# A four-layer cross-attention kernel: an earlier bias on GpSimd, a reordered layer 2, and the last layer's loads cut into pieces

## The chip, the cores and the metric

The kernel is one program on one core of a Trainium2 chip. The metric is the device time of one launch in microseconds (us), the median of several runs. TensorE (PE) does matmuls and transposes, VectorE (DVE), ScalarE (ACT) and GpSimd (POOL) do elementwise work, and SyncE (SP) issues nearly all transfers.

## The reference, cut to what matters

The model is four layers. Each adds a cross-attention and then a feed-forward block to an activation `x` of 16 x 64 rows of 512. Everything is float32.

```python
x = x + xattn0(layernorm(x), ctx)          # windowed attention
x = x + ffn0(layernorm(x))                 # int8-style SwiGLU
x = x + xattn1(layernorm(x), ctx)          # 32 heads of 128, 8 kv heads, rms norm of q and k
x = x + mxfp4(layernorm(x)) @ mxfp4(W).T + bias        # second ffn
x = x + xattn2(layernorm(x), ctx)          # 32 heads of 16, 64 queries and 64 keys a batch
x = x + topk_lora_ffn(layernorm(x))        # third ffn
x = x + xattn3(layernorm(x), cat(ctx, layernorm(x)))   # 16 heads of 96, 4 kv heads
x = x + layernorm(x) @ dequant3bit(q3, ranges).T + bias3
```

`mxfp4` takes blocks of 32 values, forms a power-of-two scale from the block's maximum and rounds each value to a 4-bit grid. `dequant3bit` is `q / 7 * (max - min) + min` with a (min, max) pair for every 32 weights. Softmax subtracts the row maximum, exponentiates and divides by the sum.

## The kernel before, in words

The activation lies in one buffer `X` of 8 tiles of 128 rows. All work is cut into *stages*: a stage has a name and an index, as `l2_s 3` for the scores of batch 3 of layer 2. `stage_order()` writes one list of all stages, `ORDER`. Each of the five engines walks through that same list and issues its own part of every stage. So the list fixes each engine's order, and the engines are bound together by semaphores alone. Every engine works in order: an instruction that waits holds up all that stands behind it on its engine.

- A matmul is three products of float32r parts, high x high, high x low and low x high. So every large weight is split after its load: ACT copies the high part (`high_parts`, L1607) and DVE subtracts it for the low part (`low_parts`, L1192).
- PSUM banks are handed out by `psum_uses`; a fill of a bank waits for the reads of the fill before it.
- **Second ffn (`f1_*`)**: for each tile DVE takes statistics, POOL makes the scale (L1979 to L1988), ACT writes the normalized rows `xn` (L1600), DVE quantizes them (`mxfp4`, nine instructions, L1197 to L1217), PE transposes (L664), ACT copies (L1807), PE multiplies (L891), and DVE adds to `X`. The bias is added to `X` on POOL (L2098). Then follow statistics, rows and transposes (L647) for layer 2. This pipeline runs beside the last steps of layer 1's attention and the first of layer 2's.
- **Layer 2's attention**: for each of 16 batches `l2_a` makes the masked keys on POOL (L2114), `l2_s` the scores on PE (L937, two banks) and on DVE the two maxima (L1432, L1435) and the subtraction for the first bank (L1440). `l2_e` exponentiates on ACT (L1853, L1860). `l2_z` takes sums and reciprocals on DVE (L1451, L1454) and multiplies on POOL (L2123). `l2_t` transposes on PE (L949), `l2_v` multiplies by the values (L960), and `l2_c` projects (L972), once for two batches. `pipe2` lists the stages of a step with their lag.
- **Layer 3's attention**: 32 units `i` (4 kv heads x 8 tiles). A step runs `l3_v i-2` (L847), `l3_a i` (L1078), `l3_t i-1` (L840), the exponentials, `l3_c i-3` (the projection, L857) and `l3_q` (a quarter of the query projections, L1059), five ahead. Heads of 96 leave quarters of partitions over, so after `l3_v` SP moves pieces inside SBUF (`o<-o`, three transfers) before `l3_c` may read. `w3` and `wo3` are the query and output weights of one kv head, 768 KB each.
- **Last ffn (`f3_*`)**: `q3`, `mn` and `mx` are its 3-bit weights and ranges. POOL rebuilds the weights piece by piece in `l3_c`, ACT and DVE split them.

SP's share of `l3_c` at index 0 is where the whole of the last ffn's inputs is issued:

```python
load(wo3[1], d["w3"][1][:, 1536:3072], D.wo3)
on.wait_ge(kv3_done.full, kv3_done.n + 1)
load(q3, d["q3"], D.f3)
for c in range(4):
    for k in range(2):
        load(range_rows(mn, c)[:, :, k, :], d["mn"][:, c, k], D.f3)
        load(range_rows(mx, c)[:, :, k, :], d["mx"][:, c, k], D.f3)
load(b3h, d["b3"], D.f3)
```

Of the kernel before, what the change touches and what calls it, by code (L numbers as in the profile page):

```python
# [17 lines left out]
NT = 8  # L18
# [42 lines left out]
def stage_order():  # L61
# [38 lines left out]
    def queries_at(u):  # L100
# [68 lines left out]
    for step, stages in enumerate(pipe2):  # L169
        order.extend(stages + kv.get(step, []))  # L170
# [24 lines left out]
def psum_uses(stage, i):  # L195
# [34 lines left out]
    if stage == "f1_turn":  # L230
        return [("p", (3,) if i < 6 else sh)]
    if stage == "f1_mm":
        return [("p", (7,) if i < 5 else sh)]
    if stage == "l2_turn":
        return [("p", (2,) if i < 4 else sh)]
# [117 lines left out]
def build_program(nc, d, out):  # L353
    ctx = ExitStack()
    with ctx:
# [42 lines left out]
        D.wo3, D.w3, D.f3, D.out = sem("d_wo3"), sem("d_w3"), sem("d_f3"), sem("d_out")  # L398
# [728 lines left out]
        def vector_program(v):  # L1127
# [295 lines left out]
            def l2_s(b):  # L1423
# [122 lines left out]
            def l3_c(i):  # L1546
# [4 lines left out]
                if 20 <= i < 24:  # L1551
                    j = i - 20
# [29 lines left out]
        def scalar_program(a):  # L1582
# [310 lines left out]
            def l3_keys(g):  # L1893
                if g == 2:
                    high_parts(w3h, w3[0], 3, D.w3, 16, S.w3h)
# [15 lines left out]
            def l3_main(_):  # L1911
                high_parts(woh3, wo3[0], 3, D.wo3, 16, S.wo3h)

            def l3_q(j):
# [11 lines left out]
                if part == 3 and g % 2 and g < 7:  # L1926
                    high_parts(w3h, w3[g // 2 + 1], 3, D.w3, 16 * (g // 2 + 2), S.w3h)
# [16 lines left out]
            def l3_c(i):  # L1944
                h, t = divmod(i, NT)
                if t == NT - 1 and h < 3:
                    w = PSUM["l3_c", i, "p"]
                    on.wait_ge(w.full, w.n + 1)
                    high_parts(woh3, wo3[h + 1], 3, D.wo3, 16 * (h + 2), S.wo3h)
                if 20 <= i < 24:  # L1950
# [494 lines left out]
```

## Time and profile before

| | us |
|---|---|
| median of 3 runs | 1686.17 (1682.86 to 1687.11) |
| the profiled execution's own time | 1683.93 |
| its span, first to last instruction | 1682.1 |
| PE busy | 1575.3 (94%) |
| DVE busy | 823.6 (49%) |
| ACT busy | 752.8 (45%) |
| POOL busy | 517.1 (31%) |
| mean granted TensorE clock | 0.979 |

A unit of PE's time that is not busy is a time in which PE stood with its next instruction still waiting. The granted clock is the share of full speed (2.4 GHz) that the chip let TensorE have; its other level is 1.2 GHz, so a mean of 0.9 over a stretch is a fifth of it at the lower level. In the profile a row names the engine, the line of the kernel, the operation, what it writes and reads, and in brackets how long the engine had been idle before it and who ended that.

### The profile page before, as it was taken

Reading aid. Unit: us, or ns where it says so; the run is one execution under the profiler, and the core shown is the slowest. Engines: PE = TensorE matmul, PEld = TensorE weight load, DVE = VectorE, ACT = ScalarE, POOL = GpSimd, SP = SyncE. Lnnn points to the kernel's source line nnn. Section 1 sums busy time; section 2 is a strip of 40 time slices with the busy share of each in tenths; the row PEclk is TensorE's granted clock in tenths of the full one; section 3 lists DMA queues with packets and bytes.
Section 4 is the critical chain, followed back from the end, with each engine's and each line's share of the span. In section 5 each row is a group of like instructions: output and inputs, shape, how many; then the busy total and the mean of one; then the engine's idle time right before and its main releaser. Section 6 shows DMA issues by size and latency. Waiting matters only on the chain. (4 is left out here: it accounts for less than half of the span.)

```text
span 1682.1 us, 25955 instructions
## 1 busy us (share of the span) xinstructions
PE 1575.3 (94%) x9522; PEld 1286.6 (76%) x9522; DVE 823.6 (49%) x1697; ACT 752.8 (45%) x2529; POOL 517.1 (31%) x648
## 2 busy tenths in 40 slices
PE   6999897789999999999999999779999999899998
PEld 5877776678888888888888888556555577787886
DVE  4566655354444454554444437755655312242454
ACT  3445443445454544544544455344333212454551
POOL 5666654132222222222222224333321000133323
PEclk9999999999999999999999999889999999999999
DMA  7000000102010010101010110011000001320101
GB/s 235 15 7 8 7 1 13 51 1 94 26 39 26 8 39 19 39 26 39 26 38 26 39 51 1 29 44 38 8 1 0 25 5 51 108 60 21 43 21 57
DMA packets 42942, 58.22 MB, mean 35 GB/s; under 512 B 26064, under 2 KB 33616, under 8 KB 39872
## 3 DMA queue, kind: packets, MB, share of 16 engines
q1 hardware_dynamic: 41136, 56.05, 10.4%
q8 instruction: 76, 1.25, 0.3%
q10 hardware_dynamic: 1616, 0.51, 0.1%
q14 instruction: 50, 0.41, 0.1%
q0 software_dynamic: 64, 0.00, 0.0%
HBM read 48.94 MB, written 2.10 MB: 30 GB/s over the span
## 5 line engine op out<-in xcount | busy, mean ns | idle before, releaser
L1727 ACT ACTIVATE big<-pb 128x128 f32<-128x128 f32 x384 | 106.6, 278 | 310.1 <-PE pb L793 202.7
L2089 POOL TENSOR_TENSOR big<-big 128x512 f32<-128x512 f32 x96 | 99.9, 1041 | 274.4 <-DVE big L1376 274.0
L1778 ACT ACTIVATE big<-pb,big 128x128 f32<-128x128 f32 x384 | 136.1, 368 | 68.8 <-issue 43.7
L1371 DVE TENSOR_REDUCE big<-pb 128x4 f32<-128x512 f32 x96 | 65.9, 686 | 174.7 <-PE pb L832 167.4
L808 PE MATMUL pb<-wkh,CXh 128*128 128x256 f32 x512 | 149.5, 292 | 1.5 <-DVE big L1361 1.5
L808 PE MATMUL pb<-wkl,CXh 128*128 128x256 f32 x512 | 144.3, 282 | 0.0
L808 PE MATMUL pb<-wkh,CXl 128*128 128x256 f32 x512 | 143.6, 281 | 0.0
L2079 POOL TENSOR_SCALAR big<-big 128x6 f32<-128x6 f32 x64 | 13.0, 204 | 424.3 <-ACT big L1727 423.7
L1166 DVE TENSOR_TENSOR X<-X,pb 128x512 f32<-128x512 f32 x128 | 86.9, 679 | 87.5 <-PE pb L1014 36.0
L857 PE MATMUL pb<-woh,oh 128*128 128x512 f32 x256 | 113.1, 442 | 3.0 <-DVE wol L1192 2.9
L793 PE MATMUL pb<-wqh,CXh 128*128 128x512 f32 x256 | 103.1, 403 | 10.6 <-DVE wql L1192 5.1
L793 PE MATMUL pb<-wqh,CXl 128*128 128x512 f32 x256 | 102.1, 399 | 0.0
L793 PE MATMUL pb<-wql,CXh 128*128 128x512 f32 x256 | 102.0, 398 | 0.0
L857 PE MATMUL pb<-woh,ol 128*128 128x512 f32 x256 | 101.7, 397 | 0.0
L857 PE MATMUL pb<-wol,oh 128*128 128x512 f32 x256 | 100.3, 392 | 0.0
L847 PE MATMUL pb<-big 128*128 128x256 f32 (+1 forms) x384 | 99.9, 383 | 0.0
L808 PEld LDWEIGHTS pb<-wkh,CXh 128*128 128x128 f32 x512 | 96.6, 189 | 2.3 <-DVE big L1361 1.8
L808 PEld LDWEIGHTS pb<-wkh,CXl 128*128 128x128 f32 x512 | 96.8, 189 | 0.0
L808 PEld LDWEIGHTS pb<-wkl,CXh 128*128 128x128 f32 x512 | 96.5, 188 | 0.3 <-issue 0.2
L1361 DVE COPY big<-pb 128x512 f32<-128x512 f32 x56 | 38.7, 690 | 104.5 <-PE pb L820 104.0
L2084 POOL TENSOR_TENSOR big<-big,half 128x6 f32<-128x6 f32 x64 | 85.0, 1328 | 9.4
L857 PE MATMUL pb<-woh,o 128*128 128x512 f32 x192 | 71.6, 428 | 7.8 <-DMA o<-o 7.5
(256 smaller groups left out, 3922.0 us busy)
## 6 DMA issues: line engine op xcount, KB each, us to landing
big<-in_w SPq DMA_DIRECT2D x17, 1024.0 KB, 4.9
big<-in_w SPq DMA_DIRECT2D x8, 768.0 KB, 5.0
big<-in_w SPq DMA_DIRECT2D x8, 512.0 KB, 3.5
o<-o SPq DMA_DIRECT2D x96, 32.0 KB, 1.9
X<-in_x SPq DMA_DIRECT2D x8, 256.0 KB, 5.7
big<-in_cn SPq DMA_DIRECT2D x8, 256.0 KB, 2.7
CXlf<-in_cT SPq DMA_DIRECT2D x8, 256.0 KB, 5.3
big<-in_wa SPq DMA_DIRECT2D x1, 2048.0 KB, 8.0
```

Of the source, the lines that this page charges most:

```text
L793: a = pe.matmul(bank(p), x_rows(x, c, t), y[:, 512 * c:512 * c + 512], start=(n == 0), stop=(n == 11))
L808: a = pe.matmul(bank(p)[:, s * 256:s * 256 + 256], kv_rows(x, c, 2 * t + s), y[:, 256 * c:256 * c + 256], start=(n == 0), stop=(n == 11), ...
L847: a = pe.matmul(bank(p)[0:hd, s * 256:s * 256 + 256], v_of(s), pt[:, s * 256:s * 256 + 256], start=(s == 0), stop=True, skip_group_check=True)
L857: a = pe.matmul(bank(p), x[:, 128 * c:128 * c + 128], y[:, 512 * c:512 * c + 512], start=(n == 0), stop=(n == 3 * size - 1))
L1166: v.tensor_tensor(X[:, t, :], X[:, t, :], bank(p), ADD).then_inc(p.free, 1)
L1361: v.tensor_copy(QT[i % 2].rearrange("p (b h q) -> p h b q", b=2, h=4), bank(p).rearrange("p (h b q) -> p h b q", h=4, b=2)).then_inc(p.fre ...
L1371: v.tensor_reduce(m[j % 2], quarters(bank(p)), AX, MAX, negate=True).then_inc(S.m, 1)
L1727: y = a.activation(sq[i % 2], bank(p)[:, j * width:j * width + 128], ACT.Square, accum_out=ss[i % 2][:, first + j:first + j + 1])
L1778: y = a.activation(e_[:, c], bank(p)[:, c], ACT.Exp, bias=m[j % 2][:, k:k + 1], scale=1.0, accum_out=z[j % 2][:, k:k + 1])
L2079: g.tensor_scalar(ss[i % 2][:, 0:6], ss[i % 2][:, 0:6], 1.0 / 128, 1e-6, MUL, ADD).then_inc(*on.to(S.pool))
L2084: g.tensor_tensor(rr[i % 2][:, 0:6], ss[i % 2][:, 0:6], half[:, 0:6], ALU.pow).then_inc(*on.to(S.rr))
L2089: g.tensor_tensor(quarters(e_), quarters(e_), bc(r[j % 2], 128), MUL).then_inc(*on.to(S.pn))
```

## The change

1. The bias of the second ffn on POOL waits until ACT has written the tile's rows, no longer until DVE has quantized them. The pipeline of that ffn gets an empty stage, `f1_wait`, between the quantizing and its transpose.
2. In layer 2 `l2_z` moves from the head of a step to behind `l2_s`, and the second ffn's step from ahead of `l2_a` to behind it. Inside `l2_s` DVE takes the first bank's maximum, subtracts, and then takes the second bank's maximum. A few PSUM tables follow.
3. `l3_turn` goes behind the values and keys of its step in layer 3's start.
4. The loads of 768 KB become three of 256 KB each, issued in several steps. The last ffn's inputs are loaded in four groups over sixteen steps, not at once, and its weights are rebuilt two steps later.
5. Layer 3's queries run six steps ahead, and the last ffn's stages are woven in after two stages of a step.

```diff
-    f1 = ["f1_stats", "f1_norm", "f1_quant", "f1_turn", "f1_mm", "l2_stats", "l2_rows", "l2_turn"]
-    ffn1 = pipeline([2 * t for t in range(NT)], [(s, every) for s in f1], ("f1_quant",))
+    f1 = ["f1_stats", "f1_norm", "f1_quant", "f1_wait", "f1_turn", "f1_mm", "l2_stats", "l2_rows", "l2_turn"]
+    ffn1 = pipeline([2 * t for t in range(NT)], [(s, None if s == "f1_wait" else every) for s in f1], ("f1_quant",))
...
-    pipe2 = batch_steps(16, [("l2_z", 3, every), ("f2_rows", 7, odd), ("l3_rows", 12, odd), ("f2_o", 11, odd),
+    pipe2 = batch_steps(16, [("f2_rows", 7, odd), ("l3_rows", 12, odd), ("f2_o", 11, odd),
...
-                             ("l2_v", 5, every), ("l2_t", 4, every), ("l2_s", 2, every), ("ffn1", 0, every),
-                             ("l2_a", 1, every), ("l2_e", 2, every), ("l2_q", 0, queries_at), ("f2_a", 8, odd),
+                             ("l2_v", 5, every), ("l2_t", 4, every), ("l2_s", 2, every), ("l2_z", 3, every),
+                             ("l2_a", 1, every), ("ffn1", 0, every), ("l2_e", 2, every), ("l2_q", 0, queries_at), ("f2_a", 8, odd),
...
-        order.extend(stages + kv.get(step, []))
+        turns = [s for s in stages if s[0] == "l3_turn"]
+        order.extend([s for s in stages if s not in turns] + kv.get(step, []) + turns)
...
-    order.extend([("l3_q", 4), ("l3_keys", 3)])
+    order.extend([("l3_q", 4), ("l3_q", 5), ("l3_keys", 3)])
...
-        if step + 5 < 4 * NT:
-            stages.append(("l3_q", step + 5))
+        if step + 6 < 4 * NT:
+            stages.append(("l3_q", step + 6))
...
-            together(stages, (ffn3, 0), (ffn3, len(stages)))
+            together(stages, (ffn3, 2), (ffn3, len(stages)))
...
                 on.mark(v.tensor_reduce(m2[2 * b % 4], b0, AX, MAX, negate=True))
-                first = on.n
-                on.wait_ge(p1.full, p1.n + 1)
-                v.tensor_reduce(m2[(2 * b + 1) % 4], b1, AX, MAX, negate=True).then_inc(S.m2, 1)
...
-                on.wait_ge(S.dve, first)
+                on.wait_ge(S.dve, on.n)
                 v.tensor_tensor(sm[2 * b % 6].rearrange("p (g k) -> p g k", g=8), b0, bc(m2[2 * b % 4], 64),
                                 ADD).then_inc(p0.free, 1)
+                on.wait_ge(p1.full, p1.n + 1)
+                v.tensor_reduce(m2[(2 * b + 1) % 4], b1, AX, MAX, negate=True).then_inc(S.m2, 1)
...
             def f1_quant(t):
-                on.wait_ge(S.mx4, 4 + t + 1)
+                rows_made(on, "f1", t)
...
+            def load_piece(h, k):
+
+                dst, landed = (w3, D.w3) if k < 3 else (wo3, D.wo3)
+                load(dst[h][:, 512 * (k % 3):512 * (k % 3) + 512], d["w3"][h][:, 512 * k:512 * k + 512], landed)
...
+                if part < 3 and g in (2, 4):
+                    on.wait_ge(S.w3l, 3 * (g // 2 + 1))
+                    load_piece(g // 2 + 1, part)
...
+                if h < 3 and 3 <= t < 6:
+                    on.wait_ge(S.wo3l, 3 * (h + 1))
+                    load_piece(h + 1, t)
+
+                j, part = divmod(i - 2, 4)
+                if 0 <= j < 4:
                     on.wait_ge(kv3_done.full, kv3_done.n + 1)
...
+                    if part == 0:
+                        load(q3[:, 512 * j:512 * j + 512], d["q3"][:, 512 * j:512 * j + 512], D.f3[j])
+                    elif part < 3:
                         for k in range(2):
...
+                            if part == 1:
+                                load(range_rows(mn, j)[:, :, k, :], d["mn"][:, j, k], D.f3[j])
+                            else:
+                                load(range_rows(mx, j)[:, :, k, :], d["mx"][:, j, k], D.f3[j])
```

Lines of the kernel after the change stand two further down than before in TensorE's part and up to `mxfp4`, and one further down in most of ACT's and POOL's.

How the order moves, at three places. First POOL, where layer 2 begins; `L2098` (after: `L2099`) is the bias of the ffn's last tile, `L2114` (`L2115`) the masked keys, `L2123` (`L2124`) the multiplication of `l2_z`. Before:

```order
467 L2114 TENSOR_TENSOR big<-big 128x256 [waits ln_rstd,d_masks,bank1_free]
468 L2098 TENSOR_TENSOR X<-X,big 128x512 [waits l2_k_masked,mxfp4]
469 L2114 TENSOR_TENSOR big<-big 128x256 [waits x_bias]
470 L2123 TENSOR_TENSOR big<-big 128x512 [waits l2_k_masked,l2_reciprocal]
471 L2123 TENSOR_TENSOR big<-big 128x512 [waits l2_probs,l2_reciprocal]
```

POOL at the same place after the change:

```order
464 L2115 TENSOR_TENSOR big<-big 128x256 [waits ln_rstd,d_masks,bank1_free]
465 L2115 TENSOR_TENSOR big<-big 128x256 [waits l2_k_masked]
466 L2099 TENSOR_TENSOR X<-X,big 128x512 [waits l2_k_masked,ln_rows_act]
467 L1980 TENSOR_SCALAR ve<-mv 128x1 [waits x_bias,ln_stats]
468 L1983 TENSOR_TENSOR rs<-ve,half 128x1 [waits pool_step]
469 L1989 TENSOR_SCALAR ve<-mv,rs 128x1 [waits pool_step]
470 L2124 TENSOR_TENSOR big<-big 128x512 [waits ln_rstd,l2_reciprocal]
471 L2124 TENSOR_TENSOR big<-big 128x512 [waits l2_probs,l2_reciprocal]
472 L2115 TENSOR_TENSOR big<-big 128x256 [waits l2_probs,bank2_full]
```

The second batch's keys now stand ahead of the last bias, and that bias waits for the rows (`ln_rows_act`) in place of the quantizing (`mxfp4`). From the third batch on the keys stand behind two multiplications whose sums come after the scores.

Second, DVE from the sums of batch 0 to the scores of batch 1, before:

```order
1089 L1451 TENSOR_REDUCE big<-big 128x8 [waits l2_exp]
1090 L1454 RECIPROCAL big<-big 128x8 [waits dve_step]
1091 L1451 TENSOR_REDUCE big<-big 128x8 [waits bank2_free]
1092 L1454 RECIPROCAL big<-big 128x8 [waits dve_step]
1093 L1432 TENSOR_REDUCE big<-pb 128x8 [waits bank1_full]
1094 L1435 TENSOR_REDUCE big<-pb 128x8 [waits bank2_full]
1095 L1440 TENSOR_TENSOR big<-pb,big 128x512 [waits dve_step]
```

The same two stages after the change:

```order
1088 L1434 TENSOR_REDUCE big<-pb 128x8 [waits bank1_full]
1089 L1439 TENSOR_TENSOR big<-pb,big 128x512 [waits dve_step]
1090 L1442 TENSOR_REDUCE big<-pb 128x8 [waits bank2_full]
1091 L1452 TENSOR_REDUCE big<-big 128x8 [waits l2_exp]
1092 L1455 RECIPROCAL big<-big 128x8 [waits dve_step]
1093 L1452 TENSOR_REDUCE big<-big 128x8 [waits bank2_free]
1094 L1455 RECIPROCAL big<-big 128x8 [waits dve_step]
```

The sums of one batch now follow the maxima of the next one, and the subtraction that releases the first exponential stands between the two maxima.

Third, SP in layer 3, where `o_0` and `o_1` are the moves after `l3_v`, `in_w` a weight load and `in_q`, `in_mn`, `in_mx` the last ffn's inputs. Before (the `in_mn` and `in_mx` rows go on to 16, then `in_b`, then the next `o_0`):

```order
93 L2174 DMA big<-in_w 128x1536 [waits w3_low]
94 L2174 DMA o_1<-o_1 32x2x128 [waits bank5_free]
95 L2174 DMA o_1<-o_1 32x2x128 x2
96 L2174 DMA big<-in_w 128x1536 [waits wo3_low]
97 L2174 DMA big<-in_q 128x2048 [waits bank3_full]
98 L2174 DMA CXhf<-in_mn 128x2x128
99 L2174 DMA CXlf<-in_mx 128x2x128
```

SP over the same units after the change:

```order
96 L2176 DMA big<-in_w 128x512 [waits w3_low]
97 L2176 DMA o_1<-o_1 32x2x128 [waits bank5_free]
98 L2176 DMA o_1<-o_1 32x2x128 x2
99 L2176 DMA big<-big 32x8x64 [waits bank0_free]
100 L2176 DMA big<-in_w 128x512
101 L2176 DMA o_0<-o_0 32x2x128 [waits bank5_free]
102 L2176 DMA o_0<-o_0 32x2x128 x2
```

Between the moves of two units there is now one piece of a weight and one query move, where eighteen issues of the last ffn's inputs and a whole weight stood.

## Rows read from the trace of the kernel before

**Rows 1.** Busy time by stretch: start:end length, PE, PEld, DVE, ACT, POOL, clock, DMA, GB/s.
```profile
1010.00:1104.00 94.00, 81.80 (x435) 66.34 (x435) 62.89 (x126) 44.17 (x132) 33.91 (x59) 0.93 0.04 13
1104.00:1166.00 62.00, 47.76 (x269) 32.58 (x266) 40.41 (x90) 29.72 (x92) 24.06 (x33) 0.89 0.09 35
1166.00:1360.00 194.00, 193.14 (x815) 109.86 (x814) 96.42 (x262) 63.43 (x162) 36.48 (x63) 1.00 0.04 14
...
1460.00:1520.00 60.00, 53.13 (x261) 43.76 (x260) 20.97 (x38) 27.20 (x91) 17.63 (x16) 0.90 0.21 57
...
1620.00:1682.10 62.10, 52.59 (x248) 40.78 (x247) 31.16 (x59) 15.31 (x49) 21.07 (x27) 0.97 0.13 44
```

**Rows 2.** PE's waits in all: line <- releaser: us in total, times, longest.
```profile
PE pb L937 <- POOL big L2114: 10.5, 2, 7.8
PE pb L857 <- DMA o<-o: 7.5, 4, 4.4
...
PE pb L664 <- DVE big L1217: 7.3, 4, 3.5
...
PE pb L647 <- ACT xn L1600: 5.1, 4, 1.4
```

**Rows 3.** Timeline of PE: one group of 32 query matmuls, twice (start, length, row).
```profile
1093.44 9.61 PE L916 MATMUL pb<-CXhf,big 128*128 128x256 f32 x32
...
1165.89 7.07 PE L916 MATMUL pb<-CXhf,big 128*128 128x256 f32 x32
```

**Rows 4.** Timeline of POOL and PE where layer 2 begins.
```profile
1111.59 1.26 POOL L2098 TENSOR_TENSOR X<-X,big 128x512 f32<-128x512 f32 x1 [13.90 <-DVE big L1217]
1112.93 0.61 POOL L2114 TENSOR_TENSOR big<-big 128x256 f32<-128x256 f32 x1
1113.60 2.08 PE L937 MATMUL pb<-big,CXlf 64*128 64x256 f32 x8 [7.82 <-POOL big L2114]
```

**Rows 5.** Timeline from one batch's scores to the next one's, PE, DVE and ACT.
```profile
1125.90 1.14 PE L937 MATMUL pb<-big,CXlf 64*128 64x256 f32 x8
1127.07 0.69 DVE L1432 TENSOR_REDUCE big<-pb 128x8 f32<-128x512 f32 x1 [6.04 <-PE pb L937]
1128.28 0.68 DVE L1440 TENSOR_TENSOR big<-pb,big 128x512 f32<-128x512 f32 x1
1129.53 1.73 ACT L1860 ACTIVATE big<-pb,big 128x64 f32<-128x64 f32 x8
1131.40 1.13 PE L937 MATMUL pb<-big,CXlf 64*128 64x256 f32 x8 [1.69 <-ACT big L1860]
```

**Rows 6.** Timeline later in layer 2: sums on DVE, POOL's multiplications, PE's light step.
```profile
1200.71 0.68 DVE L1451 TENSOR_REDUCE big<-big 128x8 f32<-128x512 f32 x1
1201.77 2.23 POOL L2123 TENSOR_TENSOR big<-big 128x512 f32<-128x512 f32 x2 [7.45 <-DVE big L1454]
1209.33 1.14 PE L937 MATMUL pb<-big,CXlf 64*128 64x256 f32 x8
1215.09 1.09 PE L949 MATMUL pb<-ident,big 128*128 128x128 f32 x8
1216.12 1.13 PE L937 MATMUL pb<-big,CXlf 64*128 64x256 f32 x8
```

**Rows 7.** Timeline of SP and PE in layer 3's attention.
```profile
1450.60 0.43 SPq L2174 DMA_DIRECT2D big<-in_q  x1
1462.60 1.87 SPq L2174 DMA_DIRECT2D o<-o  x3
1465.81 0.79 PE L857 MATMUL pb<-woh,o 128*128 128x512 f32 x1 [4.43 <-DMA o<-o]
1515.67 0.79 PE L857 MATMUL pb<-woh,o 128*128 128x512 f32 x1 [1.97 <-DMA o<-o]
```

**Rows 8.** DMA issues: count, KB each, median us from issue to landing.
```profile
big<-in_w SPq DMA_DIRECT2D x8, 768.0 KB, 5.0
...
o<-o SPq DMA_DIRECT2D x96, 32.0 KB, 1.9
```

More of the change, by code:

```diff
@@ L397, in build_program @@
         D.q3, D.o3 = [[sem(f"d_{n}3_{k}") for k in range(2)] for n in "qo"]
-        D.wo3, D.w3, D.f3, D.out = sem("d_wo3"), sem("d_w3"), sem("d_f3"), sem("d_out")
+        D.wo3, D.w3, D.b3, D.out = sem("d_wo3"), sem("d_w3"), sem("d_b3"), sem("d_out")
+        D.f3 = [sem(f"d_f3_{k}") for k in range(4)]
         banks = [ctx.enter_context(nc.psum_tensor(f"pb{i}", [128, 1024], F32)) for i in range(4)]
@@ L1948, in l3_c @@
                     on.wait_ge(w.full, w.n + 1)
-                    high_parts(woh3, wo3[h + 1], 3, D.wo3, 16 * (h + 2), S.wo3h)
-                if 20 <= i < 24:
-                    j = i - 20
+                    high_parts(woh3, wo3[h + 1], 3, D.wo3, 48 * (h + 2), S.wo3h)
+                if 22 <= i < 26:
+                    j = i - 22
                     on.wait_ge(S.w3f, j + 1)
@@ L2128, in l3_c @@
             def l3_c(i):
-                if 4 <= i < 20:
-                    j, part = divmod(i - 4, 4)
+                if 6 <= i < 22:
+                    j, part = divmod(i - 6, 4)
                     w = w3f[:, 512 * j:512 * j + 512]
                     low = range_rows(mn, j)
-                    on.wait_ge(D.f3, 288)
+                    on.wait_ge(D.f3[j], 80)
                     on.wait_ge(*on.last)
@@ L2147, in l3_c @@
                         g.tensor_tensor(w, w, low, ADD).then_inc(*on.to(S.w3f))
-                if i == 20:
+                if i == 22:
+                    on.wait_ge(D.b3, 16)
                     on.wait_ge(*on.last)
@@ L2269, in l3_begin @@
                 on.wait_ge(l2_done.full, l2_done.n + 1)
-                load(w3[0], d["w3"][0][:, 0:1536], D.w3)
+                for k in range(3):
+                    load_piece(0, k)
             def l3_keys(g):
@@ L2281, in l3_main @@
                 on.wait_ge(f2_done.full, f2_done.n + 1)
-                load(wo3[0], d["w3"][0][:, 1536:3072], D.wo3)
+                for k in range(3, 6):
+                    load_piece(0, k)
                 on.wait_ge(S.w3l, 3)
-                load(w3[1], d["w3"][1][:, 0:1536], D.w3)
+                for k in range(3):
+                    load_piece(1, k)
             def l3_q(j):
                 g, part = divmod(j, 4)
-                if part == 0:
-                    return
-                p, c = PSUM["l3_q", j - 1, "p"], part - 1
-                on.wait_ge(p.free, p.n + 1)
-                load(q3_heads(g, third(c))[:, :, 3, :], q3_heads(g, last)[:, :, c, :], D.q3[g % 2])
-                if part == 3 and g % 2 and g < 5:
-                    on.wait_ge(S.w3l, 3 * (g // 2 + 2))
-                    load(w3[g // 2 + 2], d["w3"][g // 2 + 2][:, 0:1536], D.w3)
+                if part:
+                    p, c = PSUM["l3_q", j - 1, "p"], part - 1
+                    on.wait_ge(p.free, p.n + 1)
+                    load(q3_heads(g, third(c))[:, :, 3, :], q3_heads(g, last)[:, :, c, :], D.q3[g % 2])
+                if part < 3 and g in (2, 4):
+                    on.wait_ge(S.w3l, 3 * (g // 2 + 1))
+                    load_piece(g // 2 + 1, part)
             def l3_v(i):
@@ L2306, in l3_c @@
                 h, t = divmod(i, NT)
-                if i == 0:
-                    on.wait_ge(S.wo3l, 3)
-                    load(wo3[1], d["w3"][1][:, 1536:3072], D.wo3)
+                if h < 3 and 3 <= t < 6:
[3 more added lines that the diff above has]
+                if 0 <= j < 4:
                     on.wait_ge(kv3_done.full, kv3_done.n + 1)
-                    load(q3, d["q3"], D.f3)
-                    for c in range(4):
+                    if part == 0:
+                        load(q3[:, 512 * j:512 * j + 512], d["q3"][:, 512 * j:512 * j + 512], D.f3[j])
+                    elif part < 3:
                         for k in range(2):
-                            load(range_rows(mn, c)[:, :, k, :], d["mn"][:, c, k], D.f3)
-                            load(range_rows(mx, c)[:, :, k, :], d["mx"][:, c, k], D.f3)
-                    load(b3h, d["b3"], D.f3)
-                if t == NT - 1 and h < 2:
-                    on.wait_ge(S.wo3l, 3 * (h + 2))
-                    load(wo3[h + 2], d["w3"][h + 2][:, 1536:3072], D.wo3)
+                            if part == 1:
+                                load(range_rows(mn, j)[:, :, k, :], d["mn"][:, j, k], D.f3[j])
+                            else:
+                                load(range_rows(mx, j)[:, :, k, :], d["mx"][:, j, k], D.f3[j])
+                if i == 18:
+                    load(b3h, d["b3"], D.b3)
             def end(_):
```

14 lines of the change are left out of this document (7 added, 7 removed).

## The prediction, made before the changed kernel was run

> **What bounds the kernel now.** I read the profile in this order: the page for the shares, busy time by stretch for where PE is idle, PE's waits for who ends them, and then timelines of the three places the change touches.
>
> PE is the bound. Of the 1682.1 us span it is busy 1575.3, and the change takes no matmul away. So only two things can be won: PE's idle time, and work done at TensorE's lower clock level. Both lie in few places [rows 1]. From 1010 to 1104 us (the second ffn beside the end of layer 1) PE is idle for 94.0 - 81.8 = 12.2 us at a granted clock of 0.93. From 1104 to 1166 (start of layer 2) it is idle for 14.2 us at 0.89. From 1166 to 1360 only 0.9 us is idle, at 1.00: nothing to win there, only to lose. From 1460 to 1520 (layer 3) it is idle 6.9 us at 0.90, and in the last 62 us for 9.5 us. The waits have names [rows 2]: PE's scores of layer 2 wait 10.5 us for POOL's masked keys, the projection of layer 3 waits 7.5 us for moves inside SBUF, the ffn's transposes wait 7.3 us for DVE's quantizing, and the transposes of normalized rows 5.1 us for ACT.
>
> What the lower level costs is seen directly: 32 equal matmuls took 9.61 us right after a wait and 7.07 us at full clock [rows 3]. A granted clock of c over a stretch loses at most (1 - c) of it; PE being busy only a share of the stretch, I count that share.
>
> **Part 1, the quantizing gets a step of slack (1010 to 1104 us).** The transpose of a tile stood one step behind its quantizing and waited 7.3 us in 4 waits [rows 2]. Now a step of PE work of several us lies between. DVE is busy 62.9 of the 94 us [rows 1], so it can follow a faster PE, though not by much more. Gone: 7.3 us. About 1.0 of the row waits (5.1 in all) goes as well. Given back: the transpose and the matmul of a tile stand next to each other in two steps where layer 1's work has run out, about 1.0 us in all for the copy between them. Clock: (1 - 0.93) x 94 x (81.8/94) = 5.7 us, and I let 5.4 go. Sum -12.7 us. Ends: -16 if POOL's freed queue also spares smaller waits, -4 if DVE's chain of quantizing sets the pace instead and the clock does not come back.
>
> **Part 2, POOL's bias (start of layer 2).** The last bias waited 13.90 us on POOL for the quantizing; behind it stood the second batch's keys, and PE waited 7.82 us for them [rows 4]. In the new order the keys stand ahead. What is late next is the first batch's exponential, which frees the second bank. From the scores' start to the next start that chain took 1131.40 - 1125.90 = 5.5 us [rows 5]; the early subtraction takes one DVE operation of 0.6 us out of it. Between the two scores PE has 1.1 us of scores and, by my estimate from the small transposes in the new order, 1.3 us of other work, so a wait of 2.5 us stays. So -7.82 + 2.5 = -5.3 us.
>
> **Part 3, the sums behind the maxima (layer 2).** This edit has a price. A batch's sums and POOL's multiplications now start after the next batch's maxima, the transposes need them before the scores after that, and the next keys on POOL stand behind them too. The chain from one scores' start to the next: DVE begins at +1.17, three operations take 1.9 (1127.07 to 1128.96) [rows 5], the first sum and reciprocal take 1201.77 - 1200.71 = 1.06, POOL's two multiplications 2.23 [rows 6], a gap of 0.1 and the keys 0.61 [rows 4]. Sum 7.1 us. Where a step has a query group or the third ffn beside it, PE has more than 7.1 us of work and nothing is seen. Three early light steps (batches 2 to 3, 3 to 4, 5 to 6) took 5.5, 6.1 and 5.5 us before (the first of them is in [rows 5]), so they grow by 1.6 + 1.0 + 1.6 = 4.3 us. Five later light steps hold a projection and took 1216.12 - 1209.33 = 6.79 us [rows 6]; they grow by 0.35 each, 1.8 us. The two maxima's exchange is worth nothing in them, since POOL's chain now ends last. Sum +6.1 us. Ends: +0 if the transposes' wait hides it, +20 under the first rival. The clock of 0.89 in this stretch I leave as it is: old gaps go and new ones of 3 us come.
>
> **Part 4, the row transposes of layer 3's start.** Of the four waits in [rows 2] two lie here, near the longest of 1.4 us each: 2.9 us. Four groups of value matmuls now stand ahead of these transposes and cover ACT. -2.9 us; nothing queued behind needs them sooner. Ends 0 and -4.
>
> **Part 5, loads in pieces.** From 1450.60 to 1462.60 SP issued the last ffn's inputs, and the moves of one unit were issued only then; PE waited 4.43 us [rows 7]. Spread, SP issues per step three moves (1.87 us [rows 7]), one query move, and two or three others: it keeps up with a step of PE's projection, queries and scores. The second wait, 1.97 us [rows 7], is a move that shared the DMA rings with whole weights of 768 KB, which need 5.0 us to land against a move's 1.9 [rows 8]. With a third of the size in flight it should fit. Gone: 6.4 us. Clock in this stretch: (1 - 0.90) x 60 x (53.1/60) = 5.3 us. The queries' sixth step moves the split of the query weights out of the step that splits the output weights, hidden by PE's own work. Sum -11.7 us. Ends: -14 and +40 (second rival).
>
> The Trainium skill speaks against this part: "DMA: Bandwidth & Descriptors", section "Bandwidth", says to batch transfers to 1 MiB and more, and its section on the anatomy of one DMA gives each about 2.0 us of fixed cost. By that the 19 added transfers would cost 38 us of DMA time (an estimate from that page), which counts only if a move inside SBUF waits for it; the 1.9 us of [rows 8] for a move of 32 KB agrees with the fixed cost.
>
> **Part 6, the tail.** Queries end one step earlier, so one step near the end has a group of query matmuls less to cover the split of the last output weights, while the last ffn's rows no longer stand ahead of the maxima on DVE. Of 9.5 us idle [rows 1] I take 1.5 away; ends -4 and +3.
>
> **Sum.** -12.7 - 5.3 + 6.1 - 2.9 - 11.7 - 1.5 = -28.0 us against the profiled execution's own 1683.93, so 1655.9. The median of the runs shown stands 2.2 above that execution, so I forecast 1658.
>
> **Rivals.**
> - *Layer 2 gives it back.* The new light steps leave PE idle for some 3 us each, and after such waits PE ran 32 matmuls 2.5 us longer [rows 3]. If all eight light steps are followed by that, 8 x 2.5 = 20 us are added: 1678. For it: the clock of 0.89 beside 14 us of waits [rows 1]. Against it: five of the eight wait only 0.35 us.
> - *The clock stays low.* The waits go, but the clock terms (5.4 + 5.3 = 10.7) do not: 1669. For it: other small waits remain near by. Against it: the stretch from 1166 to 1360 has 0.9 us of waits and a clock of 1.00 [rows 1]. The Trainium skill ("TensorE: Matmul & The Clock Gate", the section on what is actually happening) says that activity releases the lower level, which points to the forecast.
> - *Slower: the moves queue behind pieces.* Pieces of weights and ranges now lie in the rings in about 20 of the 32 units. If each makes the projection wait 2.0 us, as one weight did [rows 7], that is +40 us and the change ends 12 us slower: 1698. It decides once a piece delays a move by more than the slack. Against it: a move behind a weight with 5.0 us to land was late by 1.97, so the slack is 3.0 us, and a third of the weight needs 1.7 [rows 7, 8].
> - *The change does little in part 1* because DVE's chain binds: -12.7 becomes -4, 1667.
>
> **How the numbers follow.** Forecast 0.52; clock stays or part 1 is small 0.24; layer 2 gives it back 0.12; moves queue 0.08; no net effect 0.04. About 0.3% (5 us) is what a measurement can tell from none. Faster by more: 0.52 + 0.24 + two thirds of 0.12 and a little of the rest, 0.85; within 0.06; slower 0.09. The likeliest case alone spans 1648 to 1666; for 8 in 10 I go from 1643 to 1677.
>
> **What would show it.** Right: the waits of L664 on L1217 are gone; the bias on POOL has no long wait; PE's idle time from 1010 to the first scores falls by about 7 us; intervals between scores in early light steps are about 7.1 us; the projection's waits for moves are under 1 us. Wrong: waits of the projection spread over layer 3, a granted clock still near 0.9 in the three stretches, or new PE waits for POOL's multiplications through all of layer 2.

## The result

| | before | after |
|---|---|---|
| median | 1683.33 us (5 runs, 1681.81 to 1687.11) | 1670.69 us (5 runs, 1670.39 to 1676.50) |
| profiled execution | 1683.93 us | 1670.39 us |
| span, mean clock | 1682.1 us, 0.979 | 1668.6 us, 0.989 |

The ratio of after to before is 0.9927, 95% interval 0.9906 to 0.9948. So the kernel became faster by 12.3 us; the forecast was 28 us (1658, from the 1686.17 of the three runs known then). The time lies in the forecast's range and the direction is right, but 15.7 us of the gain that was worked out are missing.

Where the 13.5 us between the two profiled executions came from, by the starts of TensorE's rows at eight places of the program, the last of them TensorE's last row. In brackets is the part that is TensorE's idle time; the rest goes with the clock, since the matmuls are the same. Every later kernel is read by the same stretches.

| stretch | before | after | part of the forecast |
|---|---|---|---|
| start to projection 58 of layer 1 (L857) | 1019.2 | -0.1 | none |
| to layer 2's first scores: second ffn | 84.4 (11.8) | -1.6 (+3.4) | 1: -12.7 |
| to the second scores | 10.0 (7.8) | -4.8 (-4.6) | 2: -5.3 |
| to the last scores of layer 2 | 153.8 (7.2) | +10.0 (+3.8) | 3: +6.1 |
| to layer 3's first projection | 181.0 (4.6) | -2.3 (-3.7) | 4: -2.9 |
| to its 17th projection | 115.2 (7.1) | -9.7 (-4.0) | 5: -11.7 |
| to the end | 114.9 (6.2) | -5.0 (-0.7) | 6: -1.5 |

The stretches of [rows 1] after the change (start:end length, PE, PEld, DVE, ACT, POOL, clock, DMA, GB/s):

```profile
1010.00:1104.00 94.00, 78.59 (x442) 63.15 (x441) 63.24 (x127) 43.46 (x132) 34.54 (x58) 1.00 0.04 13
1104.00:1166.00 62.00, 49.54 (x250) 32.67 (x250) 37.30 (x84) 30.63 (x93) 20.36 (x30) 0.86 0.09 34
1166.00:1360.00 194.00, 192.35 (x818) 109.19 (x817) 99.42 (x269) 66.00 (x164) 39.33 (x67) 1.00 0.04 14
1460.00:1520.00 60.00, 58.62 (x312) 49.18 (x311) 23.30 (x42) 31.35 (x104) 16.45 (x16) 1.00 0.27 76
```

The granted clock came back to 1.00 in the second ffn and in layer 3, as forecast; at the start of layer 2 it is 0.86, a little lower than the 0.89 before. But beside the second ffn TensorE is idle 94.0 - 78.6 = 15.4 us, 3.2 more than before, not 7 less. Its waits in all, against [rows 2] (line <- releaser: us in total, times, longest):

```profile
PE pb L951 <- POOL big L2124: 9.2, 5, 3.4
PE pb L859 <- DVE wol L1194: 7.0, 4, 2.8
...
PE pb L859 <- DVE X L1168: 5.0, 4, 1.7
...
PE pb L666 <- ACT big L1769: 3.1, 2, 1.6
...
PE pb L859 <- DMA o<-o: 2.2, 1, 2.2
```

The old names are gone or small: the transposes no longer wait for the quantizing, the scores no longer for masked keys, GpSimd's bias waits 1.1 us in all, and the moves cost 2.2 in place of 7.5 us. Those 2.2 us are one wait, of the projection before the last, and more than the 1 us that the forecast had named as a sign of being right. New names stand in their place (of the second row 2.8 us lie in layer 1, 4.1 in layer 3). The timeline of TensorE, ScalarE and VectorE shows two that the forecast did not have:

```profile
1028.78 0.49 ACT L1769 ACTIVATE big<-pb,nw 128x256 f32<-128x256 f32 x1
...
1029.41 0.38 PE L666 MATMUL pb<-identb,big 128*128 128x128 bf16 x4 [1.57 <-ACT big L1769]
...
1033.42 1.03 PE L893 MATMUL pb<-big 128*128 128x512 bf16 x4
...
1036.23 0.68 DVE L1168 TENSOR_TENSOR X<-X,pb 128x512 f32<-128x512 f32 x1
...
1036.96 0.50 PE L859 MATMUL pb<-woh,oh 128*128 128x512 f32 x1 [1.65 <-DVE X L1168]
```

The ffn's transpose (L666) waits for ScalarE's copy of layer 1's keys, with which it has nothing to do but the PSUM bank: both fill bank 3. Layer 1's projection (L859) waits for the ffn's product (L893) to be added: both fill bank 7. Before, TensorE had neither of these two waits in this stretch.

In the early light steps of layer 2, which answer to [rows 5], TensorE now waits for GpSimd's multiplications, behind sums that stand behind the next maxima:

```profile
1122.31 0.68 DVE L1442 TENSOR_REDUCE big<-pb 128x8 f32<-128x512 f32 x1
1122.90 0.68 DVE L1452 TENSOR_REDUCE big<-big 128x8 f32<-128x512 f32 x1
...
1123.96 2.23 POOL L2124 TENSOR_TENSOR big<-big 128x512 f32<-128x512 f32 x2 [6.85 <-DVE big L1455]
...
1125.06 0.66 PE L951 MATMUL pb<-ident,big 128*128 128x128 f32 x4 [2.63 <-POOL big L2124]
```

In layer 3, where [rows 7] had moves behind a block of loads, SP now has one query move and one piece between two units' moves; a piece lands in 3.0 us, a whole weight took 5.0 [rows 8], and the forecast had taken 1.7 for a piece. Timeline of SP, and one row of the DMA issues:

```profile
1460.36 0.58 SPq L2176 DMA_DIRECT2D big<-big  x1
1460.99 0.60 SPq L2176 DMA_DIRECT2D big<-in_w  x1
1462.68 1.86 SPq L2176 DMA_DIRECT2D o<-o  x3
```

```profile
big<-in_w SPq DMA_DIRECT2D x24, 256.0 KB, 3.0
```

### The profile page after: what moved, and what is told of

It reads as the page before. It is cut to its first block and busy times, and to the rows that moved or that the text cites. A ratio compares the mean times of both kernels' runs of the same rounds, so it can differ in the third digit from the quotient of the medians.

```text
span 1668.6 us, 25980 instructions
## 1 busy us (share of the span) xinstructions
PE 1565.1 (94%) x9522; PEld 1276.6 (77%) x9522; DVE 822.3 (49%) x1697; ACT 754.2 (45%) x2529; POOL 516.7 (31%) x648
## 5 line engine op out<-in xcount | busy, mean ns | idle before, releaser
L1373 DVE TENSOR_REDUCE big<-pb 128x4 f32<-128x512 f32 x96 | 65.9, 686 | 178.9 <-PE pb L834 170.7
L859 PE MATMUL pb<-woh,oh 128*128 128x512 f32 x256 | 111.8, 437 | 8.0 <-DVE X L1168 5.0
L859 PE MATMUL pb<-woh,ol 128*128 128x512 f32 x256 | 101.1, 395 | 0.0
L859 PE MATMUL pb<-wol,oh 128*128 128x512 f32 x256 | 99.6, 389 | 0.0
L1980 POOL TENSOR_SCALAR ve<-mv 128x1 f32<-128x1 f32 x64 | 14.3, 224 | 249.3 <-DVE mv L1150 245.5
```

The lines of the kernel that those rows point to most:

```text
L859: a = pe.matmul(bank(p), x[:, 128 * c:128 * c + 128], y[:, 512 * c:512 * c + 512], start=(n == 0), stop=(n == 3 * size - 1))
L1373: v.tensor_reduce(m[j % 2], quarters(bank(p)), AX, MAX, negate=True).then_inc(S.m, 1)
```

## The experiments

Kernels named a_ start from the one after the change, b_ from the one before. All gains are from the ratio to before, which ran beside each; 0.1% is 1.7 us.

**a_banks.** The two tables of banks exchanged:

```diff
     if stage == "f1_turn":
-        return [("p", (3,) if i < 5 else sh)]
+        return [("p", (7,) if i < 5 else sh)]
     if stage == "f1_mm":
-        return [("p", (7,) if i < 5 else sh)]
+        return [("p", (3,) if i < 5 else sh)]
```

> The kernel after the change, with two PSUM banks exchanged for tiles 0 to 4: the second ffn's transposes (f1_turn) fill bank 7 and its products (f1_mm) fill bank 3. Theory: in the new order each of these two stands right behind or right ahead of a stage of layer 1 that fills the same bank, so TensorE waits 3.1 us for the copy of K out of bank 3 (two waits of 1.57 us) and 5.0 us for VectorE's addition out of bank 7 (1.65, 1.66, 0.74 and 0.95 us). With the banks exchanged these waits go and the time falls by 5 to 8 us, to about 1664 us. Rival: VectorE's chain of quantizing, or the chain of one tile, sets the pace of this stretch; then the waits come back under another name and the time stays within 2 us of 1670.7.

Measured: 1666.92 us, ratio 0.9908 (0.9889 to 0.9927), 3.2 us less than after; the intervals overlap, so the trace must carry it. There the stretch of the second ffn is 77.7 us, 5.1 less than after's 82.8, and both kinds of wait above are gone. That exchange changes nothing but the two banks, so this trace puts their price at 5.1 us. TensorE's longest waits in the stretch now:

```profile
PE pb L893 <- ACT big L1808: 2.7, 3, 1.4
PE pb L666 <- DVE X L1168: 1.9, 2, 1.6
PE pb L795 <- DVE big L1343: 1.5, 1, 1.5
PE pb L904 <- DVE big L1343: 1.0, 1, 1.0
PE pb L649 <- ACT xn L1601: 0.9, 1, 0.9
```

Of 8.1 us of waits 5.1 came back as time; the rest is there under other names. The largest of them, 1.9 us, is again a shared bank: the transposes of two late tiles now fill bank 7 and wait for the projection in it to be added to `X`. The others are for VectorE (L1343, 1.0 us more than in after) and ScalarE's rows (0.9).

**a_nowait.** The empty stage taken out, and two PSUM tables put back to their values of before:

```diff
-    f1 = [..., "f1_quant", "f1_wait", "f1_turn", "f1_mm", ...]
+    f1 = [..., "f1_quant", "f1_turn", "f1_mm", ...]
```

> The kernel after the change, without the empty stage between the quantizing and its transpose (its two bank tables go back as well). The forecast's own term said that this stage is worth 12.7 us: the time would be 1683 us. What the trace after shows is a loss of 7 us up to 1046 us and a win of 9 us behind it, so by the theory of the shared banks the stage is worth 2.5 us net and the time is about 1673 us: the waits for the quantizing are back (7 us), those for the shared banks are gone (8 us), and the last tiles come late again.

Measured: 1680.6 us, 0.9979 (0.9964 to 0.9994). The empty stage is worth 8.8 us, not 2.5: reading its value off one stretch was wrong. It wins 2.8 us in the second ffn's stretch, 3.3 us between the second and the third scores, since the last tile's quantizing is no longer late there, and 2.1 us on the way to layer 3's first projection. In this pair of traces another 2.8 us lie ahead of projection 58, which is within what the clock alone moves there (last section). Without it, in the other new order, the waits are longer than before (7.3 us):

```profile
PE pb L666 <- DVE big L1219: 11.1, 5, 4.5
```

**a_light and a_load.** What holds the second ffn once the banks are apart? From a_banks, first two operations of the quantizing left out (1.4 us a tile), then the same engine made lighter elsewhere:

```diff
-                on.mark(v.scalar_tensor_tensor(e3, bc(ex, 32), 0.25, e3, MUL, MAX))
-                on.wait_ge(S.dve, on.n)
...
-                on.mark(v.scalar_tensor_tensor(r4, e4, -K5, r4, MUL, ADD))
-                on.wait_ge(S.dve, on.n)
```

> The kernel a_banks with two of the nine operations of the quantizing left out (the lower bound of the step and the subtraction that ends the rounding, 1.4 us of VectorE's work for each tile), so what is quantized is not rounded. Theory: with the banks apart, what remains of TensorE's waits in the second ffn (9.6 us) is the distance from transpose to copy to product and ScalarE's rows, and VectorE's load is off the path: the time stays within 1.5 us of a_banks (1666.9). Rival, the forecast's own: VectorE's chain of quantizing sets the pace of this stretch, as it stands ahead of layer 1's maxima, whose scale GpSimd makes and VectorE then applies (waits of 1.54 and 1.03 us of TensorE); then 3 to 6 us are won.

```diff
-                on.mark(v.bn_stats(st[:, n % 4, :], X[:, t, :]))
+                cols = 128 if kind == "l2" else 512
+                on.mark(v.bn_stats(st[:, n % 4, :], X[:, t, 0:cols]))
...
+                m = 1 if i >= 58 else 4
+                v.tensor_tensor(lo[:, :, 0:m], ...[:, :, 0:m], hi[:, :, 0:m].bitcast(F32),
```

> The kernel a_banks with VectorE's load made lighter outside the quantizing: the low part of layer 1's attention output for its last units (index 58 on) is computed for a quarter of the heads only, and layer 2's statistics are taken over a quarter of the columns (1.0 us of VectorE's work for each tile by their 0.66 and 0.69 us), so both are incomplete. The chain of a tile from its rows over quantizing and transpose to the product keeps its length. Theory: after the trial with the statistics first changed nothing, VectorE's load as a whole sets the pace of the second ffn once the banks are apart; then about 1.0/1.4 of what the lighter quantizing won comes here too, 4 to 6 us faster than a_banks' 1666.9. Rival: what counted there was the length of one tile's own chain; then less than 1.5 us is won.

Measured: a_light 1661.14 us, 0.9844 (0.9820 to 0.9868), 10.8 us less than a_banks; a_load 1665.26 us, 0.9884 (0.9861 to 0.9907), 4.0 us less, with overlapping intervals. The stretch from projection 58 to the first scores, in a_banks, a_light and a_load (columns as in [rows 1]):

```profile
1019.40:1097.10 77.70, 68.06 (x363) 54.49 (x365) 56.62 (x111) 36.33 (x105) 32.17 (x56) 0.98 0.05 16
```

```profile
1025.00:1094.30 69.30, 66.03 (x367) 53.88 (x365) 46.16 (x97) 36.28 (x105) 31.64 (x55) 1.00 0.05 18
```

```profile
1020.90:1095.30 74.40, 66.55 (x365) 53.62 (x364) 53.47 (x111) 36.34 (x105) 33.06 (x56) 1.00 0.05 17
```

77.7, 69.3 and 74.4 us: 8.4 us less with 10.5 us of VectorE's busy time taken away, 3.3 us less with 3.1. VectorE is busy only 73% here and yet sets the pace, and I read the rows as a ring: layer 1's row maxima (L1373) and scaling (L1343) stand behind a quantizing of 5.7 us, the scaling waits another 2.3 to 3.2 us for GpSimd's scale, and TensorE waits for the scaling. VectorE in a_banks:

```profile
1038.04 0.68 DVE L1199 TENSOR_REDUCE big<-xn 128x16 f32<-128x512 f32 x1
...
1043.03 0.69 DVE L1219 SCALAR_TENSOR_TENSOR big<-big 128x512 bf16<-128x512 f32 x1
...
1045.32 0.66 DVE L1373 TENSOR_REDUCE big<-pb 128x4 f32<-128x512 f32 x1
1049.22 0.69 DVE L1343 TENSOR_TENSOR big<-pb,big 128x512 f32<-128x512 f32 x1 [3.24 <-POOL big L2085]
```

My theory for a_light fell; the forecast's fourth rival holds, and more was won than a_light's expectation gave it. a_load gave less than its expectation, as its two edits took 0.8 us a tile and not 1.0, but for each us taken it won as much as a_light, though a tile's own chain kept its length. That speaks for the engine's load; since its interval overlaps that of a_banks, a part for the chain is not excluded.

**best3.** The same question from the side of the order, on best2 (below): the quantizing last in its step.

```diff
-    ffn1 = pipeline(..., ("f1_quant",))
+    ffn1 = pipeline(..., ("l2_turn", "l2_rows", "l2_stats", "f1_mm", "f1_turn", "f1_norm", "f1_stats"))
```

> The kernel best2, and in a step of the second ffn's pipeline the quantizing stands last, no longer first; so VectorE takes the statistics of the two other tiles ahead of it. Leaving out 1.4 us of quantizing for each tile won 8.5 us in this stretch, more than TensorE's waits on it showed. Theory: not VectorE's load itself but its order binds: behind the quantizing stand two statistics, on GpSimd the two scales wait for them (5.19 us) and hold up layer 1's own scale, which VectorE's scaling of the queries waits for, and TensorE for that (1.52 and 1.06 us in best2). With the statistics first these two waits go and the time falls by 2 to 5 us, to about 1650 us. Rival: the load binds; then each tile's quantizing ends 1.7 us later, the waits of the transposes for it come back, and nothing is won or up to 4 us lost.

Measured: 1654.19 us, 0.9818 (0.9799 to 0.9837), the same as best2. The two waits for L1343 did go (2.6 us), and this came in their place, a wait of layer 2's first queries for VectorE's copy out of a bank in `l2_a`, which stands behind a quantizing that now ends later:

```profile
PE pb L921 <- DVE big L1424: 3.3, 1, 3.3
```

Here another order of the same work moved the wait, and less work removed it.

**a_zhead.** The sums of layer 2 back at the head of a step:

```diff
-    pipe2 = batch_steps(16, [("f2_rows", 7, odd), ...
-                             ... ("l2_s", 2, every), ("l2_z", 3, every),
+    pipe2 = batch_steps(16, [("l2_z", 3, every), ("f2_rows", 7, odd), ...
+                             ... ("l2_s", 2, every),
```

> The kernel after the change, with layer 2's sums (l2_z) back at the head of a step; the exchange of the second maximum and the subtraction stays, and so does the later place of the second ffn's step. Theory: the 10.1 us that the stretch of layer 2 gained over before (waits of TensorE's transposes for GpSimd's multiplications, 2.63, 2.12 and 3.37 us, and about 0.5 us in each later light step) are the price of this move alone; they go, and the time falls by 8 to 10 us, to about 1661 us. Rival: the sums ahead of the maxima hold up the subtraction and with it the first bank, so waits for ScalarE's exponential take their place; then the time falls by less than 4 us.

Measured: 1661.45 us, 0.9867 (0.9850 to 0.9884), 10.1 us less than after. From the second to the last scores it takes 153.9 us, where after took 163.9 and before 153.8. So the whole +10.0 us of that stretch is the price of this one move; the rival is excluded. What is left in its place is small, three waits for ScalarE's exponential of 1.5 to 2.2 us, where before had three of 1.7 to 2.7 (two of them for ScalarE). One of them:

```profile
1123.55 1.14 PE L939 MATMUL pb<-big,CXlf 64*128 64x256 f32 x8 [1.60 <-ACT big L1861]
```

**b_bias.** On the kernel before, GpSimd's bias alone:

```diff
             def f1_quant(t):
-                on.wait_ge(S.mx4, 4 + t + 1)
+                rows_made(on, "f1", t)
```

> The kernel before the change, with the bias of the second ffn on GpSimd waiting for the written rows and no longer for the quantizing, and nothing else. By the forecast the wait of 7.82 us for the second batch's keys falls to 2.5 us or less, and the time falls by about 5 us, to 1678 us. Rival: the keys are early, but the next wait for the bank's exponential grows by the same amount, and the time stays at 1683 us. A second rival: GpSimd's queue is freed all through the second ffn and more than 5 us are won.

Measured: 1685.49 us, 1.0004 (0.9991 to 1.0018): no gain. Yet in its trace the wait of 7.82 us is down to 3.25 us, now for ScalarE's exponential, and the stretch between the first two scores 4.6 us shorter. By the eighth scores 3.0 us are gone again: the stretch from the fourth to the eighth is that much longer with the same idle time. Start:end length, PE, clock, DMA share, GB/s, of before and then of b_bias. Its first scores start at 1110.1 us, where those of before start at 1103.6, so the same times are not quite the same work; cut from its own first scores on, the two stretches of 20 us have clocks of 1.00 and 0.83.

```profile
1104.00:1124.00 20.00, 12.18 (x58) 0.74 0.00 1
1124.00:1144.00 20.00, 15.65 (x106) 1.00 0.28 106
```

```profile
1104.00:1124.00 20.00, 15.02 (x78) 1.00 0.00 1
1124.00:1144.00 20.00, 15.50 (x93) 0.84 0.28 106
```

In before the lower level fell beside the long wait; in b_bias it fell later, beside work. These are one trace of each kernel.

**b_maxima.** On the kernel before, the subtraction ahead of the second maximum alone:

```diff
-                first = on.n
-                on.wait_ge(p1.full, p1.n + 1)
-                v.tensor_reduce(m2[(2 * b + 1) % 4], b1, AX, MAX, negate=True).then_inc(S.m2, 1)
...
                 v.tensor_tensor(sm[2 * b % 6].rearrange("p (g k) -> p g k", g=8), b0, bc(m2[2 * b % 4], 64),
                                 ADD).then_inc(p0.free, 1)
+                on.wait_ge(p1.full, p1.n + 1)
+                v.tensor_reduce(m2[(2 * b + 1) % 4], b1, AX, MAX, negate=True).then_inc(S.m2, 1)
```

> The kernel before the change, with only this edit: in layer 2's scores VectorE subtracts the first bank's maximum before it takes the second bank's. The forecast gave it 0.6 us in a light step and called it worth nothing once the sums stand behind it. Theory: in the early light steps TensorE waits for ScalarE's exponential of the first bank (1.69 and 2.08 us) and these get up to 0.6 us shorter each; in all 1 us, 1683 us, not to be told from no change. Rival: ScalarE's exponentials start earlier and the clock comes back sooner; 3 us or more.

Measured: 1680.86 us, 0.9973 (0.9962 to 0.9983), 4.5 us faster. The execution that was traced is the slowest of its ten (1685.02), so the trace can't show the whole gain. It shows 0.4 and 0.3 us less in two early light steps and 1.6 us less in the step behind them (6.8 for 8.4 us), with no idle time in either, so at a higher clock; the remaining 2 us are not shown. The size that the rival gave (3 us or more) came true; only part of its reason is seen.

**b_loads.** Everything of before but the loads:

```diff
-                load(w3[0], d["w3"][0][:, 0:1536], D.w3)
+                for k in range(3):
+                    load_piece(0, k)
...
+                if part < 3 and g in (2, 4):
+                    on.wait_ge(S.w3l, 3 * (g // 2 + 1))
+                    load_piece(g // 2 + 1, part)
...
+                if h < 3 and 3 <= t < 6:
+                    on.wait_ge(S.wo3l, 3 * (h + 1))
+                    load_piece(h + 1, t)
...
```

> The kernel before the change with the loads in pieces alone: weights in thirds, the last ffn's inputs in four groups over sixteen steps and its weights rebuilt two steps later; queries five steps ahead and the last ffn's stages woven as before. In the trace after, the stretch from the first head's projection to the end is 14.7 us shorter. Theory: the pieces alone bring 10 to 12 us of these (waits of 6.4 us and the clock beside them), so 1672 us. Against it: in the trace of the bias alone, where layer 3 is untouched, the same stretch is 3.2 us shorter than before by the clock alone, so the gain may be 8 us, 1676 us. By the fourth rival of the forecast, transfers in the rings delaying the moves, it would be slower than 1684 us, which the trace after excludes.

Measured: 1676.41 us, 0.9946 (0.9930 to 0.9963), 9.1 us faster. The first two heads' projections take 12.5 us less (6.8 of it idle time), the last stretch 3.0 us more. TensorE's three longest waits from layer 3's attention on:

```profile
PE pb L841 <- POOL big L2090: 2.7, 3, 2.3
PE pb L858 <- DMA o<-o: 2.1, 2, 1.6
PE pb L1079 <- ACT big L1779: 2.0, 2, 1.0
```

Both waits for a move lie near the end and none is spread over the projections; the third rival, which the expectation calls the fourth, is excluded. The pieces and the spreading of the last ffn's inputs were not tried one without the other.

**a_q5.** Queries five steps ahead, the ffn's stages at the head of a step:

```diff
...
-        if step + 6 < 4 * NT:
-            stages.append(("l3_q", step + 6))
+        if step + 5 < 4 * NT:
+            stages.append(("l3_q", step + 5))
...
-            together(stages, (ffn3, 2), (ffn3, len(stages)))
+            together(stages, (ffn3, 0), (ffn3, len(stages)))
```

> The kernel after the change, with layer 3's queries five steps ahead again and the last ffn's stages woven in at the head of a step as before; loads in pieces stay. By the traces of after and of the loads alone: the two changes of head before the last get 1.4 and 1.4 us faster (the projection's wait for the low parts of the output weights is not there with five steps), and the stretch of the last head gets 7 us slower, since GpSimd's and ScalarE's waits of 1.0 to 2.4 us are back there. Theory: 4 to 5 us slower than after, 1675 us. Rival, the forecast's: this part is worth 1.5 us, 1672 us.

Measured: 1676.72 us, 0.9952 (0.9937 to 0.9967), 4.2 us slower than after, with intervals that overlap. As its theory said, the first two heads are 3.1 us faster and the last stretch is 8.4 us slower. The 3.1 us belong to the queries, as the ffn's stages are woven in only behind them; for the last stretch the two edits were taken back together, so which of them earns it stays open.

**best1 and best2.** best1 is a_banks and a_zhead in one. best2 adds one edit, the projection's wait for low parts by thirds:

```diff
                 for c in range(size):
+                    if low is not None:
+                        on.wait_ge(S.wo3l, low + c + 1)
...
             def l3_c(i):
-                on.wait_ge(S.wo3l, 3 * (i // NT) + 3)
```

> The kernel after the change with both: the banks of f1_turn and f1_mm exchanged (3.8 us faster by medians alone, 5.1 us in the stretch of the second ffn) and layer 2's sums back at the head of a step (9.3 us faster alone, 9.4 us in its stretch). The two lie in stretches that follow each other. Theory: they add up, 1657 us. Rival: with an earlier start of layer 2 the last ffn tile comes late and the first batches wait for it; then the sum is 3 to 5 us short, 1661 us.

> The kernel best1, and layer 3's projection waits for the low part of the output weights one third at a time, ahead of each chunk, and no longer for all three thirds ahead of the first. In the trace after the change the projection waits 1.38, 1.67 and 1.09 us (4.1 us) for these low parts at the three changes of head, which is 3 us more than before lost there. Theory: VectorE makes a third in 0.7 to 1.1 us and a chunk takes TensorE 0.8 us, so most of each wait goes: 2 to 3.5 us faster than best1. Rival: the first third is what is late (ScalarE's copy starts only when the last tile of the head is projected), and less than 1 us is won.

Measured: best1 1653.80 us, 0.9823 (0.9800 to 0.9847); best2 1653.29 us, 0.9818 (0.9793 to 0.9843). best1 is 17.5 us faster than after, 4.2 more than its two edits alone; in its trace the clock between the first scores and 1166 us is 0.97:

```profile
1098.00:1166.00 68.00, 58.68 (x326) 40.40 (x324) 46.27 (x110) 36.32 (x109) 24.11 (x36) 0.97 0.15 55
```

After had 0.86 from 1104 to 1166 us. That the 4.2 us are this clock is not shown, as these are single traces. With best2's edit best1's 3.9 us of waits for low parts at the changes of head are gone and its profiled execution is 3.1 us shorter than best1's (1650.42 against 1653.50); by the medians the difference is 0.5 us, not to be told from none. Both beat after; best2 is the fastest in hand, 1.8% below before.

## Why the prediction was wrong, and where it was right

- **Part 1 failed**, and with it the forecast: -12.7 us forecast, -1.6 measured in its stretch, 11.1 of the 14.5 us by which the sum missed the two profiled executions. Its clock term was right (-5.4 against -5.0). Its idle term (-7.3) had the wrong sign: TensorE's idle time grew by 3.4 us. The step that failed is "Now a step of PE work of several us lies between", with nothing given back but 1.0 us. The moved stages also moved relative to layer 1's, onto neighbours that fill the same PSUM banks (5.1 us by a_banks), and VectorE could not follow a faster TensorE (up to 8.4 us by a_light). With the banks apart the stretch is 6.7 us shorter than before; the 6.0 us that are then still missing from the 12.7 are of the size of what a lighter VectorE wins. The shared banks it did not look for, although the change edits the tables of banks. The forecast had named VectorE's chain as its -4 end and its fourth rival (1667), and had put it aside because VectorE was busy "62.9 of the 94 us". Its own case of a clock that stays low (1669) is nearer to the 1670.7 measured, but by luck: in the two stretches that it speaks of, the clock did come back.  That the stage pays for itself elsewhere (8.8 us by a_nowait) was not foreseen either.
- **Part 2** was right in size and place (-4.8 against -5.3), but by itself it gives no measurable gain: in b_bias's trace 3.0 of the 4.6 us come back as time at the lower clock.
- **Part 3** was mis-sized: +6.1 forecast, +10.0 measured, all of it this move (a_zhead). The chain of 7.1 us was right, the later light steps take 7.3. Missing were the step from batch 3 to 4 (8.5 us, not 7.1) and 1.4 us for a step with queries, which the forecast took as hidden. The sum has small slips too: its own numbers give 1.6 + 1.0 + 1.6 = 4.2 and 5 x 0.3 = 1.6, so 5.8; and of the later light steps four, not five, took 6.8 us.
- **Part 4** was right: both waits of 1.45 us are gone, -2.3 in the stretch against -2.9.
- **Part 5** was right by the loads alone: -12.5 us in the two heads against -11.7. In the full change it is -9.7, as the queries' sixth step, which the forecast took as hidden, adds waits for the low parts (1.38 and 1.67 us at the first two changes of head; a_q5 has neither). The same step and the ffn's new place pay in **Part 6**: -5.0 against -1.5. The 1.7 us for a piece, which stood against the third rival, was wrong: it takes 3.0 us to land, as long as the slack that the forecast worked out, and yet it delayed no move in those two heads. Part of the clock term was this one trace of before: in b_bias and b_maxima, where layer 3 is untouched, the stretch from the ninth to the 17th projection was 3.0 and 3.1 us shorter than in the trace of before. So the match of -12.5 with -11.7 is in part luck. Here is b_bias against the clock of 0.90 in [rows 1]:

```profile
1460.00:1520.00 60.00, 53.77 (x275) 44.38 (x274) 21.66 (x39) 28.80 (x99) 17.51 (x17) 0.97 0.26 69
```

- The rival of layer 2 giving it back set 20 us on top of part 3's 6.1; measured are 3.9 on top. It was right that rows run longer: of the 10.0 us only 3.8 are idle time, and the rest is rows that run longer beside a clock of 0.86. Its size was five times too large. The Trainium skill's advice on large transfers ("DMA: Bandwidth & Descriptors", section "Bandwidth") did not hold here: the 19 added transfers did not cost 38 us, the kernel with them is 9.1 us faster. The 38 us were an estimate from that page's fixed cost, which its section on the anatomy of one DMA gives for transfers that GpSimd issues, while SP issues these. The DMA engines are busy about a quarter of the time here (0.27 in after from 1460 to 1520 us). The long wait of before was a move issued only when 12 us of other issues were through; whether that or the size of the loads counted more is not separated.

## What to carry to other kernels

When a stage is moved, list what it shares with its new neighbours, PSUM banks above all: a wait that disappears can come back under the name of a stage that has no data in common with it. An engine that is busy three quarters of a stretch can still set its pace; ask what happens to each instruction that queues behind the long block, not what its share is. Take the value of an edit from undoing it in the finished kernel, over the whole program, rather than from one stretch of one trace.

## What the runs showed of the hardware

- When a wait was shortened, the lower clock level came later instead of ending: 7.82 us of wait fell to 3.25 us, the granted clock of the 20 us beside it rose from 0.74 to 1.00, that of the next 20 us fell from 1.00 to 0.84 (one trace of each), and the time did not change measurably.
- One trace's clock is not the kernel's. The kernel before, b_loads and b_maxima are the same program up to projection 58 and took 1019.2, 1020.0 and 1026.3 us to get there, with 58.6, 62.0 and 56.3 us of TensorE's idle time, so clock terms of 3 us in one profile are within what the next shows without any edit.
